# A hybrid transformer block on one core: a new order for the first token group, for row 3 and for the side steps, and one of four copies on ScalarE

## The reference

```python
x = x + attn_a(layernorm(x), Wq, Wk, Wv, lambda_params, g1, g2, g3, W1, W2)
x = x + ffn(layernorm(x), gate_w, gate_up_w, down_w)
x = x + attn_b(layernorm(x), w_qkv, w_out, b_out)
x = x + ffn(layernorm(x), gate_w, gate_up_w, down_w)
```

## Time and profile before

| | us |
|---|---|
| three runs | 1050.1, 1046.89, 1049.34 |
| median | 1049.34 |
| the profiled execution | 1050.18 |
| its span, first to last instruction | 1048.4 |

### The profile page before, as it was taken

The page is one execution under the profiler, slowest core; times in us unless marked ns, Lnnn a source line. Parts: engine busy times, 40 slices in busy tenths (PEclk is TensorE's granted clock), DMA queues, the critical chain, the costliest instruction groups (busy, mean ns, idle before and its releaser), DMA issues.

```text
span 1048.4 us, 16649 instructions
## 1 busy us (share of the span) xinstructions
PE 938.2 (89%) x5472; PEld 649.0 (62%) x5472; DVE 646.9 (62%) x1444; ACT 609.1 (58%) x1865; POOL 657.5 (63%) x607
## 2 busy tenths in 40 slices
PE   3246999889999999999999998999999999988998
PEld 1034665568666666668666665668666666676665
DVE  5884785447775864779737854779744343576432
ACT  4246565657366557689384566689364453875432
POOL 5763778444568874857668764857655645454654
PEclk9998999866899999999999999999999999988999
DMA  5004343101435543541234433541153555011652
GB/s 176 1 0 94 80 91 73 41 2 42 103 85 119 110 104 83 121 95 43 61 83 107 106 81 84 121 94 43 41 122 82 123 122 124 19 42 28 137 123 60
DMA packets 63224, 85.67 MB, mean 82 GB/s; under 512 B 3681, under 2 KB 29090, under 8 KB 62882
## 3 DMA queue, kind: packets, MB, share of 16 engines
q1 hardware_dynamic: 63138, 84.61, 35.8%
HBM read 79.32 MB, written 5.28 MB: 81 GB/s over the span
## 4 chain that ended last, share of the span: by engine, by line
PE 63%; ACT 12%; DVE 6%; POOL 6%; issue 5%; DMA 1%; DVEq 0%; SPq 0%; ACTq 0%; POOLq 0%
PE bank L1378 17%; PE bank L1353 8%; PE bank L1355 8%; PE bank L1354 8%; ACT probs L953 4%; PE bank L1414 4%; PE bank L1399 4%; PE bank L1428 2%; POOL work L776 2%; PE bank L1392 1%; PE bank L1251 1%; PE bank L1257 1%; ACT work L933 1%; ACT L933 1%; DVE probsT L1199 1%
## 5 line engine op out<-in xcount | busy, mean ns | idle before, releaser
L776 POOL TENSOR_TENSOR work<-work,spread_w 128x512 f32<-128x512 f32 x256 | 336.8, 1327 | 186.0 <-DVE work L1158 164.9
L1158 DVE TENSOR_TENSOR work<-work,bank 128x512 f32<-128x512 f32 x256 | 174.4, 682 | 242.4 <-ACT work L933 144.3
L1378 PE MATMUL bank<-work,down_w 128*128 128x512 f32 x512 | 265.3, 602 | 10.1 <-ACT yT L945 5.6
L933 ACT ACTIVATE work<-bank 128x512 f32<-128x512 f32 x256 | 150.8, 595 | 179.4 <-PE bank L1355 175.9
L953 ACT ACTIVATE probs<-bank,neg_max 128x96 f32<-128x96 f32 x512 | 165.7, 381 | 32.5 <-DVE neg_max L1185 19.9
L1353 PE MATMUL bank<-z_hi,gate_hi 128*128 128x512 f32 x256 | 171.9, 671 | 0.0
L784 POOL TENSOR_TENSOR probs<-probs,prob_inv 128x768 f32<-128x768 f32 x64 | 94.0, 1469 | 89.5 <-DVE prob_inv L1193 89.4
L953 ACT ACTIVATION_READ_ACCUMULATOR probs<-bank,neg_max 128x1 f32 x512 | 125.2, 248 | 0.0
L1378 PEld LDWEIGHTS bank<-work,down_w 128*128 128x128 f32 x512 | 95.8, 191 | 39.8 <-POOL work L776 11.3
L1355 PE MATMUL bank<-z_hi,gate_lo 128*128 128x512 f32 x256 | 102.6, 401 | 0.0
L1353 PE MATMUL bank<-z_hi,up_hi 128*128 128x512 f32 x256 | 102.2, 399 | 0.0
(11 more groups left out here) (142 smaller groups left out, 1467.3 us busy)
## 6 DMA issues: line engine op xcount, KB each, us to landing
spread_w<-comb_dram SPq DMA_DIRECT2D x128, 512.0 KB, 6.7
vals<-v_dram SPq DMA_DIRECT2D x16, 384.0 KB, 4.2
x_buf<-x SPq DMA_DIRECT2D x8, 256.0 KB, 3.3
v_dram<-v_tok SPq DMA_DIRECT2D x8, 256.0 KB, 6.7
out<-xs SPq DMA_DIRECT2D x8, 256.0 KB, 5.1
spread_w<-wg SPq DMA_DIRECT2D x1, 1024.0 KB, 6.4
spread_w<-wu SPq DMA_DIRECT2D x1, 1024.0 KB, 8.5
comb_dram<-combT SPq DMA_DIRECT2D x16, 64.0 KB, 1.6
```

Of the source, the lines that this page charges most:

```text
L776: pool.tensor_tensor(work[:, n % WORK], work[:, n % WORK], spread_w[:, n // EACH % 2, s % EACH], ALU.mult).then_inc(hid_gated, 1)
L933: act.activation(work[:, n % WORK], bank[GATE_BANKS[ring_of(row, f, s)]], ACT.Silu).then_inc(silu_ready, 1)
L1158: dve.tensor_tensor(work[:, n % WORK], work[:, n % WORK], bank[UP_BANKS[ring_of(row, f, s)]], ALU.mult).then_inc(gated_ready, 1)
L1378: pe.matmul(bank[Y_BANK], down_w[:, c], work[:, n % WORK], start=(c == 0), stop=(c == CH - 1)).then_inc(down_done, 1)
```

## The change

1. One of the four blocks of turned probabilities, block 1 (`ACT_BLOCK`), is copied by ScalarE, between the exponentials of head groups 2 and 3 of the next tile; VectorE copies the other three. It has a semaphore of its own.
2. The first group. The projections of row 0's first four tiles go to banks 0 to 3 (`qkv_first`), and their relu, exponential, elu and scaling are done tile by tile, with a semaphore each. The weights of the projection are waited for by themselves. The splits `w_lo` 0, `w_hi` 1 and `w_lo` 1 come later in `AHEAD`, group 0's routing and the first three chunks come ahead of the norms of group 1, and the next row's norm and projections come last. The second half of the masks moves to slot 3 of row 0's "third" stage.
3. The order of row 3. Period 3 has three feed-forward stages: "fourth" (row 2, f 3) moves behind row 3's attention, ahead of (3, 2) and (3, 3). Row 3 adds into its own rows of `x_buf` and not into `xs`. The steps `y_back` 1 and `s_stats` to `values` 1 of row 3 move into its attention, its `m_` steps and routing out of it.
4. Side steps take other slots in rows 0 to 2, as the diff shows.

```diff
@@ PLAN
+ACT_BLOCK = 1
     "second": {
-        2: ahead(("qscale", 0)),
-        3: ahead(("kvsum", 0)),
+        3: ahead(("qscale", 0), ("kvsum", 0)),
     "third": {
         0: own(("seq_turn", 0)) + ahead(("wred", 3)),
-        1: own(("keys", 0)) + ahead(("x_apply", 1), ("h_sq1", 0)),
-        3: ahead(("x_turn", 1), ("h_newton1", 0)) + back(("m_stats", 3), ("m_rstd", 3)),
-        4: back(("m_apply", 3)) + ahead(("h_newton2", 0), ("h_rg", 0)),
-        5: back(("y_back", 2)) + ahead(("h_scale", 0)),
-        6: back(("moe_turn", 3), ("z_hi", 3)) + ahead(("h_sq2", 0)),
...
+        1: own(("keys", 0)) + back(("m_stats", 3), ("m_rstd", 3)) + ahead(("h_sq1", 0)),
+        3: ahead(("x_apply", 1), ("h_newton1", 0)),
+        4: ahead(("h_newton2", 0), ("h_rg", 0)),
+        5: back(("y_back", 2), ("m_apply", 3)) + ahead(("x_turn", 1), ("h_scale", 0)),
+        6: ahead(("h_sq2", 0)),
+        7: back(("moe_turn", 3), ("z_hi", 3)) + ahead(("h_red2", 0), ("h_pow2", 0)),
...
     "fourth": {
-        0: ahead(("mlp2", 0), ("elu", 1), ("attend", 4)),
-        1: ahead(("m_stats", 0), ("m_rstd", 0), ("qscale", 1)),
+        0: ahead(("qkv", 7), ("mlp2", 0)),
+        1: ahead(("expo", 1), ("elu", 1), ("attend", 4), ("m_stats", 0), ("m_rstd", 0)),
...
@@ SPECIAL
     (0, "third"): {
-        2: ahead(("expo", 1), ("elu", 1)),
-        3: ahead(("h_scale", 0), ("qscale", 1), ("attend", 4)),
+        3: ahead(("expo", 1), ("elu", 1), ("h_scale", 0), ("masks", 2)),
+        4: ahead(("qscale", 1), ("attend", 4), ("h_sq2", 0)),
...
     (ROWS - 1, "attn"): {
-        17: own(("proj", 0), ("m_stats", 2), ("m_rstd", 2)),
-        18: own(("m_apply", 2)),
-        20: own(("moe_turn", 2), ("z_hi", 2)),
...
+        3: own(("y_back", 1), ("s_stats", 1), ("s_rstd", 1)),
+        4: own(("s_apply", 1)),
+        6: own(("seq_turn", 1)),
+        7: own(("keys", 1)),
+        8: own(("queries", 1)),
+        11: own(("values", 1)),
+        26: own(("proj", 0)),
@@ AHEAD
-    ("w_lo", 0), ("w_hi", 1), ("w_lo", 1), ("x_turn", 0), ("qkv", 0), ("qkv", 1), ("x_apply", 1), ("qkv", 2), ("qkv", 3),
-    ("lam", 0), ("expo", 0), ("elu", 0), ("attend", 0), ("qscale", 0), ("attend", 1), ("x_turn", 1), ("kvsum", 0),
...
+    ("x_turn", 0), ("qkv_first", 0), ("qkv_first", 1), ("lam", 0), ("elu_first", 0), ("attend", 0), ("qkv_first", 2),
+    ("elu_first", 1), ("qkv_first", 3), ("kvsum", 0), ("elu_first", 2), ("attend", 1), ("wterm", 0), ("wred", 0),
...
+    ("route", 0), ("r_sum", 0), ("top", 0), ("weigh", 0), ("early", 0), ("wterm", 6), ("comb", 0), ("cnorm", 0),
+    ("wred", 6), ("weighT", 0), ("early", 1), ("kvsum", 7), ("lead", 0)) + ahead(("x_stats", 0), ("x_rstd", 0)) + own(
+    ("early", 2), ("wterm", 7), ("lead", 1), ("wred", 7), ("h_sq1", 1), ("lead", 2), ("h_red1", 1), ("h_newton1", 1),
+    ("h_newton2", 1), ("h_rg", 1)) + ahead(("x_apply", 0), ("x_turn", 0), ("qkv", 0)) + own(
+    ("h_scale", 1), ("h_sq2", 1), ("h_red2", 1), ("h_pow2", 1)) + ahead(("qkv", 1)) + own(
+    ("h_gain", 1), ("h_sum", 1), ("x_add", 1)) + ahead(("qkv", 2), ("qkv", 3))
@@ stages_of
+        if 0 < period < ROWS - 1:
+            yield "fourth", period - 1, G + 1
+        yield "attn", period, None
+    else:
+        yield "fourth", ROWS - 2, G + 1
+        yield "second", ROWS - 1, G
+        yield "last", ROWS - 1, G + 1
@@ scalar
+            def turned_block(row, i):
+                wait(act, mix_ready, tile(row, i))
+                act.wait_ge(probsT_ready, tile(row, i) * NB + ACT_BLOCK + 1)
+                act.activation(probsT[:, ACT_BLOCK], bank[4 + ACT_BLOCK % 2][0:KW, :], ACT.Copy)\
+                   .then_inc(probsT_copied_act, 1)
...
                         exponentials(row, i, 2)
+                        if i:
+                            turned_block(row, i - 1)
                         exponentials(row, i, 3)
@@ vector
-                            turned(row, i - 1, (0, 1))
+                            turned(row, i - 1, (0,))
```

More of the change, by code:

```diff
@@ L137 @@
+        13: back(("cnorm", 3)) + ahead(("mlp1", 0), ("qkv", 6)),
+        14: back(("weighT", 3)),
+        15: own(("queries", 0)),
     },
     "fourth": {
-        0: ahead(("mlp2", 0), ("elu", 1), ("attend", 4)),
-        1: ahead(("m_stats", 0), ("m_rstd", 0), ("qscale", 1)),
-        2: ahead(("kvsum", 4)),
-        3: own(("values", 0)) + ahead(("wterm", 4), ("attend", 5), ("wred", 4)),
-        4: ahead(("m_apply", 0)),
-        5: own(("y_back", 1)) + ahead(("kvsum", 5)),
-        6: ahead(("moe_turn", 0), ("z_hi", 0)) + own(("s_stats", 1), ("s_rstd", 1)),
@@ L155 @@
+        8: ahead(("route", 0), ("r_sum", 0), ("wred", 5)) + own(("s_apply", 1)),
+        9: ahead(("top", 0), ("kvsum", 6)),
+        10: own(("seq_turn", 1)) + ahead(("weigh", 0), ("wterm", 6), ("attend", 7)),
+        11: own(("keys", 1)) + ahead(("comb", 0), ("wred", 6)),
+        12: ahead(("cnorm", 0)) + own(("queries", 1)) + ahead(("kvsum", 7)),
+        13: ahead(("wterm", 7)),
+        14: own(("values", 1)) + ahead(("wred", 7)),
+        15: ahead(("weighT", 0)),
     },
@@ L297 @@
     },
-    (ROWS, "fourth"): {
+    (ROWS, "last"): {
         5: back(("y_back", 2)),
@@ L568, in _ @@
             load_rows(0, 0)
+            for dst, src in qkv_a_loads:
+                sp.dma_start(dst, src).then_inc(qkv_a_loaded, 16)
             load_rows(0, 1)
@@ L828, in norm_apply @@
                 k = NORM_AT[row, kind, n]
-                src = xs if kind == "m" and n >= G else x_of(row)
+                src = sum_of(row) if kind == "m" and n >= G else x_of(row)
                 act.wait_ge(rstd_ready, k + 1)
@@ L1278, in route @@
             def route(row, f):
+                if row == 0 and f == 0:
+                    pe.wait_ge(router_ready, 1)
                 side_free(row, "route", f)
```

241 lines of the change are left out of this document (142 added, 99 removed).

## The result

The change makes the kernel slower: 1074.38 us, the median of four runs (1073.05 to 1075.61), against 1049.72 of the kernel before (four runs, 1046.89 to 1052.47). The ratio is 1.0235, 95% interval 1.0204 to 1.0266, so 21 to 28 us. The forecast was 1048.9 with a range up to 1062.

The account below looks back on a forecast made before the run. TensorE was taken to set the pace, ScalarE 0.13 us a tile behind. Terms -2.6 + 4.4 + 1 + 1.5 - 2.7 - 2.1 = -0.5 gave 1049.7 from 1050.2, forecast 1048.9 us as median, range 1034 to 1062.

Parts of the forecast that it names:

- start: Before the first weighted chunk: reordered first group brings that chunk from 95.2 to 92.6, -2.6 us; bounds 0 and -8.
- copies, rows 1 and 2: Attention of rows 1 and 2: ScalarE copies lengthen steady tiles from 5.36 to 5.72 us, +4.4 us; bounds 0 and +7.8.
- copies, rows 0 and 3: Row 0's attention runs at half clock and hides the copies, +1 us; row 3's losses include 2.2 for them.
- masks: Row 0's second stage: GpSimd's 7.6 us block stalls 2 to 4.5, half made good, +1.5 us; bounds 0 and +7.6.
- side steps, rows 1 and 2: Feed-forward stages of rows 1 and 2: earlier statistics and later apply save 3.7, fourth stages add; -2.7 us, between -6 and +3.
- row 3: Row 3's attention with the moved stage behind it: losses 16.1 us against 18.2, -2.1 us.
- +0.5 for each fourth stage: Fourth stages of rows 1 and 2: the projection and exponential moved there add 0.5 us each.
- 2.2 us wait of the transpose: In the 51 us stage: a transpose's wait for banks released by VectorE would go under the new side-step order.
- path up to the first product: In the start: GpSimd's first product of keys and values begins at 16.4 in place of 24.45.
- list that holds the first chunk back: In the start: GpSimd's strict order keeps the second group's sum into x ahead; of 8 to 15 us, 2.6 remain.
- Old and new alike have four tiles of VectorE work behind it: In the start: after the first product, VectorE's work still takes 18.8 us, ending at 35.2, 8 us earlier.
- recorded rival of half clock in row 3: Row 3's attention: waits for applied norm and keys' copy renew half clock, +7 to +10 us, 1055 to 1059; chance 0.18.

Follow-up runs that it names:

- experiment 10: Kernel before plus row 3's new order, the new start, and the masks' block in row 0's second stage: 1060.04 us, ratio 1.0068.
- experiment 3: Kernel before with only the second of the four turned-probability copies moved to ScalarE: 1060.84 us, ratio 1.0105.
- experiment 4: Changed kernel without GpSimd's block of masks in row 0's second stage (output values change): 1070.68 us, ratio 1.0193.
- experiment 11: Kernel before plus row 3's new order and new side steps of rows 1 and 2, weights' turning left at slot 13: 1050.96 us, ratio 1.0017.
- experiment 6: Kernel before with the new order of row 3 alone: 1047.31 us, ratio 0.9983.
- experiment 9: Kernel before plus row 3's new order and row 0's new side steps, masks still in the start: 1044.8 us, ratio 0.9940.
- Experiment 1: Changed kernel with the turning of the next row's weights back at slot 13 of the fourth stages, from 15: 1062.86 us, ratio 1.0132.
- experiment 12: Kernel before with only the turning of the next row's weights moved from slot 13 to 15, rows 1 and 2's fourth stages: 1051.33 us, ratio 1.0008.
- experiment 5: Changed kernel with the weights' turning back at slot 13 and all four copies back on VectorE: 1056.54 us, ratio 1.0080.
- experiment 7: Kernel of experiment 5 with the masks in four pieces in row 0's first stage, not one block in its second: 1055.42 us, ratio 1.0061.
- experiment 8: Kernel of experiment 5 with row 0's second-group sum into x moved behind GpSimd's third weighted chunk, its reader one slot later: 1059.79 us, ratio 1.0111.
- experiment 13: Kernel of experiment 10 without GpSimd's subtraction for the gate weights' low part (high part multiplied instead): 1047.47 us, a single run.
- experiment 2: Changed kernel with all four copies of turned probabilities on VectorE again: 1061.9 us, ratio 1.0103.

## Why the prediction was wrong

| term | predicted | measured |
|---|---|---|
| start | -2.6 | +3.3 in the trace, +2.7 in experiment 10 |
| copies, rows 1 and 2 | +4.4 | +3.2 in the profile of experiment 3 |
| copies, rows 0 and 3 | +1, and 2.2 of row 3's losses | 8, the rest of experiment 3's 11 |
| masks | +1.5 | +3.7 by the medians, +4.7 in the profile (experiment 4) |
| side steps, rows 1 and 2 | -2.7 | +3.6 at slot 13 (experiment 11 against 6); slot 15 another 11.5 with the copy |
| row 3 | -2.1 | -2.1 (experiment 6; interval -4.6 to +0.9) |
| row 0's side steps | not priced | -2.5 (experiment 9 against 6; -4.5 by the ratios) |

*Side steps of rows 1 and 2: the step that failed, and the largest.* The prediction priced what moves within the stages ("+0.5 each" for the fourth stages) and never took up that the turning of the next row's weights moves to slot 15, the slot behind which ScalarE changes its table. A stage's last slot is not free when the engine has a switch to make there. Experiment 1 settles it: 11.5 us in this kernel. It is not the price of the slot by itself (experiment 12: 1.3 us), and what makes the fall behind the gaps long is not known.

The other half of the term was wrong too. Its +0.5 for each fourth stage measured +2.3 and +1.2 (43.6 and 42.5 us in experiment 11, and within 0.2 of that in experiments 1, 5, 7 and 8, against 41.2). And the 2.2 us wait of the transpose was to go; in row 2's third stage after the change there is a wait of 2.4 us in its place, with 3.4 us of half clock behind it as before, and the stage takes 50.7 us in place of 51.1:

```profile
PE bank L1326 <- DVEq L1177: 2.4, 1, 2.4
```

What the prediction blamed is gone. ScalarE waited 4.39 us for the norm's shift before (605.06), and after the change it applies the norm at 614.55 without a wait. But a transpose now stands in the same slot as `y_back` 2 and needs the bank that VectorE's add frees. VectorE comes to that add only behind its own steps of the next row's head norm, one of which takes 1.27 us while GpSimd runs a weighted chunk (614.82 to 616.09), and 0.23 the next time. ScalarE before, then ScalarE and VectorE after:

```profile
605.06 1.65 ACT L834 ACTIVATE z<-xs,shift,rstd 128x128 f32<-128x128 f32 x4 [4.39 <-POOL shift L735]
```

```profile
614.55 1.64 ACT L874 ACTIVATE z<-xs,shift,rstd 128x128 f32<-128x128 f32 x4
```

```profile
614.91 1.27 DVE L1141 SCALAR_TENSOR_TENSOR head_rms<-newton,head_rms 128x64 f32<-128x64 f32 x1
...
616.73 0.23 DVE L1141 SCALAR_TENSOR_TENSOR head_rms<-newton,head_rms 128x64 f32<-128x64 f32 x1
...
617.47 0.68 DVE L1174 TENSOR_TENSOR xs<-xs,bank 128x512 f32<-128x512 f32 x1
```

*The copies.* In the steady tile the mechanism was right and the size a little high: +0.36 us a tile predicted, +0.25 measured; the two calm stages +4.4 against +3.2. For rows 0 and 3 together 3.2 us were set down ("the copies are hidden there", and 2.2 in row 3), and the timed cost of the copy alone leaves 8. A stage at half clock was taken for one in which ScalarE's work can't matter. In the profile of experiment 3 the half clock of these two attentions is 7 and 10 us longer, which at half speed is 3 and 5 us of their 4.4 and 5.1; so most of it looks like clock. That is one profile: row 0's part varies by 8 us in profiles of identical code (124.7 to 132.7), and row 3's attention took 76.2 us in experiment 12 where it took 73.5 before, so how the 8 us divide isn't settled. The Trainium skill, TensorEngine Tiling (Array Packing), section PSUM Bottleneck, has ScalarE share the emptying of the banks. The prediction set it aside since TensorE is the last to finish here, and 11 us more in experiment 3 bear that out.

*The start.* The path up to the first product was right (16.4 predicted, 16.07 in the trace), and so was the list that holds the first chunk back (the sum into x at 97.28, the chunk at 98.50). What failed is "Old and new alike have four tiles of VectorE work behind it", with the old 18.8 us. GpSimd's low split moved from 13.97, ahead of the chain, to 29.29, into it, and held VectorE up for 4 us: 39.82 in place of 35.2 for the fourth tile, 84.6 in place of 78.5 for the eighth. In experiment 13 they are 35.69 and 80.6, and the first chunk comes at 94.5 and not at 92.6; so 4 us of the miss are the split's, and 2 more, most of them lost between the fourth and the eighth tile, stay open. The prediction says that the change "takes the large weight splits away from ahead of it" and doesn't ask where they land. The row was there to read: 4.91 us for a cast that takes 1.23 alone, next to GpSimd's 4.51. The Trainium skill says it as a rule, in SBUF — State Buffer, section SBUF: two separate sides: VectorE and GpSimd share a pair of ports as an exclusive lock, held for a whole instruction by whichever comes first; it bears on a VectorE instruction that reads two operands from SBUF against a GpSimd instruction that reads there, and on one of VectorE in a mode that uses two ports. The traces agree for the product, which reads two: 4 us here, gone in experiment 13. The cast reads one and was held up alike; which mode it ran in no run here shows.

*The masks.* The block came where and as long as predicted (7.2 us from chunk 3 on). The stall of TensorE was 4.7 us where "2 to 4.5, half made good" was said, and nothing of it was made good: the stage takes 5.1 us more with the block than without it (experiment 4), 6.0 more than with the masks in pieces (experiment 7), and the attention behind it is the same in both pairs. The rest of the stage's 9.4 us is not the masks: with row 0's new side steps and no block it takes 42.3 (experiment 9) in place of 39.0. Why the attention behind it was shorter than before the change isn't settled. It spent 34 us at half clock in place of 55, but so it did in experiment 11, whose row 0 has the old steps.

*Row 3.* Right in sign and size, as far as ten runs tell, and in part by luck. The prediction had 9.1 us idle and 7 of clock in that attention; experiment 6 has 6.7 idle (65.28 busy of 72) and two falls of 10.2 us at half clock, some 10 lost, 16.9 in place of 16.1. The idle time was less and the clock dearer. In the changed kernel TensorE's waits in that attention are the two that were named, the keys' copy and the applied norm, and each has 10 us of half clock behind it:

```profile
PE bank L1398 <- ACT keysT L865: 2.0, 1, 2.0
...
PE bank L1326 <- ACT z L874: 1.1, 1, 1.1
```

The Trainium skill, TensorE: Matmul & The Clock Gate, section HAM oscillation, tells of a loop that its waits throttle again and again; the waits that it tells of are longer than these. Here each of the two waits has a fall of its own behind it: the granted clock is 0.53 from 898 to 909 and from 912 to 923. The recorded rival of half clock in row 3 had such falls; they came, 3 us dearer than the 7 of the sum, and less idle time made up for it. The long fall came in row 2, behind two gaps and with no further wait in its 24 us, where the prediction saw nothing to set it off.

*The sum.* From the changed kernel down by the timed medians: slot -11.5, copies -6.3, and the 7 us that are left over the kernel before are the start, the masks and the side steps of rows 1 and 2 against the gains of rows 0 and 3. The single terms of experiments 6, 9, 10 and 11 add to +11.7 by the medians and to +6 by the ratios, against 7 and 8 for experiment 5; with intervals of some 3 us on each, these runs can't tell whether the terms add. The copies and the slot seem not to: together they cost 17.8 us, one by one in the changed kernel 12.5 and 11.5.

## What to carry to other kernels

A step moved to the edge of a stage must be read against what its engine does first in the next one: a table load hides behind the last silu only as long as nothing that waits for another engine stands between them. Work taken off the front of a chain is still somewhere; look at what the two engines do beside each other at its new place, in a row of the old trace where they were together before. A change made of several moves is best timed move by move: the two that gain here (row 0's steps and row 3's order, 0.6% together) were hidden under those that lose.

## What the runs showed of the hardware

- A VectorE product of 1.23 us takes 5.26 beside GpSimd's subtraction of 4.50, and a cast of 1.23 us takes 4.91 beside it; without the subtraction the product takes 1.23 (experiment 13). Both end 1.1 us behind the subtraction.
- The same two gaps (1.4 and 1.0 us) at the start of an attention stage had 3.4 us of half clock behind them in row 1 and 24 us in row 2 of one execution. The long one is in the profiles of three kernels that have the gaps (after, experiments 2 and 4) and not in that of a fourth (experiment 12).
- The clock at which an unchanged part runs is not the same from one execution to the next: row 0's second stage and attention took 132.1, 132.7, 126.2 and 124.7 us with the same instructions (the kernel before, experiments 6, 12 and 11), and all of that lies in the attention; the stage took 39.0 each time. One profile can't price a term of less than 8 us in that attention.
